# Two-layer attention and routing kernel: values' tail product on four tiles of the array, second layer's side rows made by POOL

## The chip, the cores and the metric

One core of one Trainium2 chip runs the whole program. The metric is device time in microseconds (us), the median of three runs. TensorE is called PE here, VectorE DVE, ScalarE ACT, GpSimd POOL and the queue that issues most DMAs SP.

## The reference

The input x is 4 batches of 2048 tokens of width 512. Two layers follow each other, each an attention over a short context and a feed-forward part:

```
x = x + xcond(layernorm(x), ctx, ...)     # layer 0: 16 heads of 32, 154 keys per batch
x = x + moe(layernorm(x))                 # 32 experts, 8 for a token
x = x + xcond(layernorm(x), ctx, ...)     # layer 1, own weights
x = x + light_and_heavy(layernorm(x))     # light MLP for all, heavy MLP for 512 routed tokens of a batch

def xcond(q_in, ctx, tau, delta):
    q, k, v = heads(q_in @ Wq.T + bq), heads(ctx @ Wk.T + bk), heads(ctx @ Wv.T + bv)
    p = softmax((q @ k.T * tau + delta) / sqrt(32))      # over 154 keys
    return merge(p @ v) @ Wo.T + bo
```

The change touches only the two attentions (the product `p @ v`) and, in layer 1, the layernorm whose rows go to the light and heavy part.

## The kernel before

The program is a sequence of phases: keys and values of layer 0, `token_phase` for layer 0, expert slots and experts, `token_phase` for layer 1, the mixed phase and the heavy phase. `token_phase` walks over 16 turns of 512 tokens (four tiles of 128). A turn has 16 units, one for each group g of four heads and each tile t (unit u = 4g + t), and 32 slots `at`, two for each unit. The order of all work on every engine is written out by hand: each engine has a function `turn` that goes through the slots in order, and tables of slot numbers (`V`, `OL`, `RES`, `NZ`, `PT`, `OO` and others, lines 349 to 380) say in which slot a piece of work stands. Turn i works on three sets of tokens at once: the attention of turn i, the output projection of turn i - 1, the side rows of turn i - 2; V, PT, OO and OL name slots of this turn for groups 0 and 1 (and 2 for PT), and of the next turn for the rest.

One unit goes through the engines like this. PE makes the scores (L980, four heads, banks 0 to 2 of PSUM); DVE takes the maximum (L684); ACT makes the exponentials of four heads and their sums (L915); DVE the reciprocal (L699); POOL multiplies the 128 main keys (L609) and the 26 tail keys (L611) by it; PE turns the four heads of the main keys into bank 4 (L992) and the 4 x 26 = 104 tail columns into bank 5 (L993); DVE, in two of 16 units ACT, copies bank 4 to `pTm` (L707, L861). PE may use bank 4 again for unit v only when all copies up to v - 1 are done, and makes the last head of the scores of unit u only when ACT has read the first head of unit u - 1 (the semaphore `shared`). When the four units of a group are done, ACT copies bank 5 to `pTt` (L854), and PE makes the values (`values`, L1003 and L1006): one fp32 product of 104 rows, whose left operand `vt` is block-diagonal (rows of four heads, zeros off their own columns), and four fp32 products of 128 rows and 32 columns, one per head, onto the same bank 7. A product in fp32 is two MATMUL instructions in the trace. ACT (L849) and DVE (L726) take the result out as high and low part. Bank 6 holds queries and projections in turn.

In layer 1, DVE does in slots 3, 7, 10 and 13 the normalised side rows of turn i - 2 (`normed(1, "s", ...)`, L675 with output `z`) from `xs`, which the next residual (L716, slot 12, one buffer) overwrites tile by tile; they all are on DVE, so no semaphore stands between them. In the slots around it POOL has L654 (`xbo`, slots 6, 10, 16, 22) and L602 (`q_low`, slots 26, 1, 11, 15). POOL's 16 turns are a loop with waits against registers.

The constants at the top of the file that matter: `KTAIL` = 26, `HG` = 4 heads in a group, `TG` = 4 tiles, `GTOK` = 512 tokens of a turn.

Of the kernel before, what the change touches and what calls it, by code (L numbers as in the profile page):

```python
# [20 lines left out]
P = 128  # L21
B, SEQ, D = 4, 2048, 512
NTOK = B * SEQ
KEYS = 154
# [4 lines left out]
TROWS = HG * KTAIL  # L29
# [16 lines left out]
UNITS = TG * GROUPS  # L46
KROWS = 3 * DK + 2
# [121 lines left out]
def store_tails(sp, scr, l, k, s):  # L169

    for h in range(HG):
        sp.dma_start(scr[f"vt{l}"].rearrange("b (n h) (g e d) -> h (b n) g e d", h=HG, e=HG, d=DK)[h, :, :, h, :],
                     k["vt"][:].rearrange("n (g e d) -> n g e d", e=HG, d=DK)[:, :, h, :]).then_inc(s["stored"], 16)


KV_STORED = 16 * (2 * 3 * HG + 2 + HG)
# [29 lines left out]
def key_value_phase(nc, a, scr, c):  # L206

    with ExitStack() as ctx:
# [6 lines left out]
        zero = sb("zero", [TROWS, D])  # L215
# [6 lines left out]
        def _(sp):  # L222
# [7 lines left out]
            for l in range(2):  # L230
                sp.dma_start(scr[f"vt{l}"].rearrange("b t d -> t b d"),
                             zero[:].unsqueeze(1).to_broadcast([TROWS, B, D])).then_inc(s["cleared"], 16)
# [61 lines left out]
def token_phase(nc, l, a, scr, c, x_in, x_rows):  # L294
    gate = l == 0
    with ExitStack() as ctx:
# [6 lines left out]

        wq, wo = operands("wq", [P, DC, D]), operands("wo", [P, DC, D])
        bq, bo = sb("bq", [P, DC]), sb("bo", [P, D])
        kst = sb("kst", [KROWS, GROUPS, HG * KEYS], F32R)
        vm, vt = sb("vm", [P, D]), sb("vt", [TROWS, D])
# [7 lines left out]
        tails = sb("tails", [P, 4, TROWS])  # L315
        pTm, pTt = sb("pTm", [P, 2, HG, D]), sb("pTt", [TROWS, D])
        negmax, total, inv = (sb(n, [P, UNITS, HG]) for n in ("negmax", "total", "inv"))
        stat, mv = sb("stat", [P, 2, TG, 6]), sb("mv", [P, 2, TG, 2])
# [8 lines left out]
        else:  # L327
# [7 lines left out]
                 "q_mm q_out q_high q_low scored negmax shared exped inv normed p_mm pTm pTt pv oT_high oT_out proj resid "  # L335
# [4 lines left out]
        T_BANK, A_BANK, B_BANK = 3, 6, 7  # L340
# [8 lines left out]
        V = (15, 24, 2, 7) if gate else (15, 23, 3, 6)  # L349
# [4 lines left out]
        OL = (23, 30, 4, 9) if gate else (17, 27, 5, 9)  # L354
# [8 lines left out]
        NZ = (0, 0, 1, 1) if gate else (3, 7, 10, 13)  # L363
# [3 lines left out]
        PT = (11, 19, 28, 3) if gate else (11, 19, 27, 4)  # L367
        OO = (16, 26, 2, 7) if gate else (15, 24, 4, 7)
# [39 lines left out]

        def o_bank(j, t):

            return (A_BANK, 0, 1, 2)[t] if last(j) else A_BANK
# [20 lines left out]
        def load_values(sp, j, g):  # L432
# [4 lines left out]
            sp.dma_start(vt[:, g * P:(g + 1) * P], scr["vt%d" % l][b, :, g * P:(g + 1) * P]).then_inc(s[f"v_in{g}"], 16)  # L437
# [139 lines left out]
        def _(pool):  # L577
            pool.memset(half[:], -0.5).then_inc(s["ready"], 1)
            pool.memset(eps[:], EPS).then_inc(s["ready"], 1)
            if not gate:  # L580
                pool.memset(z[:, :, D:XS], 0.0).then_inc(s["ready"], 1)
                pool.memset(c["z_last"][:, :, D:XS], 0.0).then_inc(s["ready"], 1)
            pool.wait_ge(s["ready"], 2 if gate else 4)
# [21 lines left out]
            def normalize(i, v):  # L605
# [3 lines left out]
                pool.tensor_tensor(main, main, inv[:, v, :].unsqueeze(2).to_broadcast([P, HG, P]),  # L609
                                   ALU.mult).then_inc(s["normed"], 1)  # L610
                pool.tensor_tensor(tails[:, v % 4, :].rearrange("p (n h) -> p h n", h=HG), tail,  # L611
                                   inv[:, v, :].unsqueeze(2).to_broadcast([P, HG, KTAIL]),
                                   ALU.mult).then_inc(s["normed"], 1)

            def turn(i, par, prev2, prev, cur, nxt, nxt2, before, batch):
# [14 lines left out]
                for st in range(UNITS):  # L630
# [3 lines left out]
                    for at in (2 * st, 2 * st + 1):  # L634
# [21 lines left out]
            turns(pool, turn)  # L656

        @block.vector
        def _(dve):
# [37 lines left out]
            def inverse(i, v):  # L697
                dve.wait_ge(s["exped"], UNITS * i + v + 1)
                dve.reciprocal(inv[:, v, :], total[:, v, :]).then_inc(s["inv"], 1)  # L699
# [10 lines left out]
            def residual(j, t):  # L710
# [12 lines left out]
            def o_low(i, par, g):  # L723
                dve.wait_ge(s["oT_high"], GROUPS * i + g + 1)
                k = o_slot(par, g)
                dve.tensor_tensor(oT[1][:, k, :], ps[:, B_BANK, :], oT[0][:, k, :].bitcast(F32),  # L726
# [34 lines left out]
            def turn(i, par, prev2, prev, cur, nxt, nxt2, before, batch):  # L761
# [3 lines left out]
                for at in range(2 * UNITS):  # L765
# [45 lines left out]
                    if prev2:  # L811
# [1757 lines left out]
```

## Time and profile before

| what | value |
|---|---|
| median of three runs | 3376.84 us (3376.42 to 3385.39) |
| the profiled execution, its own time | 3380.68 us |
| its span, first to last instruction | 3378.9 us |
| granted TensorE clock, mean over the span | 0.978 of full speed |
| busy share PE, DVE, ACT, POOL | 95%, 81%, 46%, 62% |
| one turn of layer 0, of layer 1 | about 52.6 us, about 50.5 us |

A busy PE means that some matmul is in flight; its instructions overlap, so times of the PE work are best read from start to start in the timeline. The timeline merges neighbouring instructions of one line (`x4`); its first two columns are start and duration of the merged stretch in us.

### The profile page before, as it was taken

What the parts mean: (1) busy time and instruction counts of PE and PEld (TensorE: products, weight loads), DVE (VectorE), ACT (ScalarE), POOL (GpSimd) and SP (SyncE); (2) the same over time, 40 slices, a digit from 0 to 9 for tenths busy, and PEclk for the clock granted to TensorE, in tenths of its full rate; (3) what the DMA queues carried; (4) which work ended last, traced back from release to release, by engine and by line L of the source; (5) the groups of instructions that cost most, each with busy time, mean ns of one, the idle gap of its engine ahead of it and who ended that gap; (6) DMA issues with size and microseconds to landing.
All of it is one profiled execution on the core that took longest, in us unless ns stands there. A gap on an engine that the chain in (4) does not pass through costs nothing. (4 is left out here: it accounts for less than half of the span.)

```text
span 3378.9 us, 55655 instructions
## 1 busy us (share of the span) xinstructions
PE 3197.8 (95%) x17324; PEld 2506.5 (74%) x17324; DVE 2735.5 (81%) x5290; ACT 1560.9 (46%) x5449; POOL 2081.7 (62%) x2335
## 2 busy tenths in 40 slices
PE   7999999999979999999999699999999969999998
PEld 5677777777648888888888577777777757778886
DVE  4788888888677887888887379999999879967775
ACT  1766767667521111111111377777777745321111
POOL 1776666766536777777777477777777753443333
PEclk8999999999979999999999899999999989999999
DMA  7345454454465667676766544555554457730111
GB/s 218 100 137 173 122 166 140 137 174 125 141 174 154 171 169 175 170 166 166 176 164 156 112 128 133 160 163 143 151 172 135 138 164 286 274 103 13 26 13 25
DMA packets 284781, 490.97 MB, mean 145 GB/s; under 512 B 54018, under 2 KB 74818, under 8 KB 283778
## 3 DMA queue, kind: packets, MB, share of 16 engines
q1 hardware_dynamic: 243698, 408.87, 39.6%
q0 software_dynamic: 32256, 77.65, 12.4%
q10 hardware_dynamic: 8592, 1.57, 0.3%
q8 instruction: 116, 1.90, 0.2%
q14 instruction: 119, 0.97, 0.1%
HBM read 250.32 MB, written 136.96 MB: 115 GB/s over the span
## 5 line engine op out<-in xcount | busy, mean ns | idle before, releaser
L915 ACT ACTIVATE c_pr<-ps,t_negmax 128x154 f32<-128x154 f32 x1024 | 385.7, 393 | 180.8 <-DVE t_negmax L684 178.6
L684 DVE TENSOR_REDUCE t_negmax<-ps 128x4 f32<-128x616 f32 x512 | 403.6, 788 | 53.3 <-PE ps L980 52.6
L915 ACT ACTIVATE t_pr<-ps,t_negmax 128x154 f32<-128x154 f32 x1024 | 385.6, 393 | 105.8 <-DVE t_negmax L684 101.4
L707 DVE COPY t_pTm<-ps 128x512 f32<-128x512 f32 x448 | 306.0, 683 | 127.3 <-PE ps L993 123.0
L609 POOL TENSOR_TENSOR t_pr<-t_pr,t_inv 128x512 f32<-128x512 f32 x256 | 275.7, 1077 | 191.0 <-DVE t_inv L699 189.3
L609 POOL TENSOR_TENSOR c_pr<-c_pr,t_inv 128x512 f32<-128x512 f32 x256 | 272.0, 1063 | 196.4 <-DVE t_inv L699 195.0
L980 PE MATMUL ps<-t_kst,t_stack 98*128 98x154 f32 x2048 | 353.0, 291 | 26.3 <-DMA t_stack<-t_q_low 10.1
L980 PEld LDWEIGHTS ps<-t_kst,t_stack 98*128 98x128 f32 x2048 | 279.6, 194 | 38.9 <-issue 17.8
L81 PE MATMUL ps<-e_xT_high,e_wgu_high 128*128 128x512 f32 x768 | 302.4, 394 | 1.4 <-DVE e_xT_low L1508 1.4
L83 PE MATMUL ps<-e_xT_high,e_wgu_low 128*128 128x512 f32 x768 | 299.6, 390 | 0.0
L82 PE MATMUL ps<-e_xT_low,e_wgu_high 128*128 128x512 f32 x768 | 299.4, 390 | 0.0
L1618 ACT ACTIVATE e_sig<-ps 128x512 f32<-128x512 f32 x96 | 57.5, 599 | 516.2 <-PE ps L83 516.2
L81 PE MATMUL ps<-t_xnT_high,t_wq_high 128*128 128x512 f32 x512 | 221.3, 432 | 19.1 <-ACT t_qT L842 18.4
L2286 POOL TENSOR_TENSOR h_w_low<-c_hw,h_w_high 128x512 fp32r<-128x512 f32 x64 | 89.9, 1405 | 229.3 <-DVE h_w_high L70 229.3
L81 PE MATMUL ps<-t_wo_high,t_oT_high 128*128 128x512 f32 x512 | 217.9, 426 | 0.0
L602 POOL TENSOR_TENSOR t_q_low<-t_qT,t_q_high 128x512 fp32r<-128x512 f32 x128 | 170.7, 1334 | 68.8 <-DVE t_q_high L70 68.8
L915 ACT ACTIVATION_READ_ACCUMULATOR t_pr<-ps,t_negmax 128x1 f32 x1024 | 213.0, 208 | 0.0
L915 ACT ACTIVATION_READ_ACCUMULATOR c_pr<-ps,t_negmax 128x1 f32 x1024 | 212.4, 207 | 0.0
L1480 POOL TENSOR_TENSOR e_wd_low<-c_wd_in,e_wd_high 128x512 fp32r<-128x512 f32 x96 | 131.1, 1394 | 128.9 <-DVE e_wd_high L70 128.9
L83 PE MATMUL ps<-t_xnT_high,t_wq_low 128*128 128x512 f32 x512 | 203.0, 396 | 0.0
L82 PE MATMUL ps<-t_xnT_low,t_wq_high 128*128 128x512 f32 x512 | 202.2, 395 | 0.0
L83 PE MATMUL ps<-t_wo_high,t_oT_low 128*128 128x512 f32 x512 | 201.4, 393 | 0.0
(373 smaller groups left out, 9320.9 us busy)
## 6 DMA issues: line engine op xcount, KB each, us to landing
t_stack<-t_q_high SPq DMA_DIRECT2D x1016, 64.0 KB, 2.0
c_wgu_in<-in_gate_upT SPq DMA_DIRECT2D x32, 1536.0 KB, 6.4
t_stack<-t_q_low SPq DMA_DIRECT2D x512, 64.0 KB, 2.0
x_dram<-c_wide_rows SPq DMA_DIRECT2D x32, 1024.0 KB, 7.8
c_wd_in<-in_downT SPq DMA_DIRECT2D x32, 768.0 KB, 4.5
t_xbo<-in_x SPq DMA_DIRECT2D x16, 1024.0 KB, 7.0
xw_dram<-t_z SPq DMA_DIRECT2D x16, 1024.0 KB, 5.3
t_xbo<-x_dram SPq DMA_DIRECT2D x16, 1024.0 KB, 11.0
```

Source lines behind the costliest of these rows:

```text
L81: pe.matmul(out, left[0], right[0], start=start, stop=False)
L82: pe.matmul(out, left[0], right[1], start=False, stop=False)
L83: return pe.matmul(out, left[1], right[0], start=False, stop=stop)
L602: pool.tensor_tensor(qlow[:, n % 2, :], qT[:, n % 2, :], qhigh[:, n % 2, :].bitcast(F32), ALU.subtract).then_inc(s["q_low"], 1)
L609: pool.tensor_tensor(main, main, inv[:, v, :].unsqueeze(2).to_broadcast([P, HG, P]), ALU.mult).then_inc(s["normed"], 1)
L684: dve.tensor_reduce(negmax[:, u, :], flat[:, at:at + HG * APART].rearrange("p (h n) -> p h n", h=HG)[:, :, 0:KEYS], AX, ALU.max, negate=Tr ...
L707: dve.tensor_copy(pTm[:, g % 2, :, t * P:(t + 1) * P], ps[:, 4, :].rearrange("p (h n) -> p h n", h=HG)).then_inc(s["pTm"], 1)
L915: op = act.activation(pr[:, u % 4, h, :], flat[:, col:col + KEYS], ACT.Exp, bias=negmax[:, u, h:h + 1], accum_out=total[:, u, h:h + 1])
L980: mm = pe.matmul(flat[:, at:at + KEYS], stack[:, HG * (g % 2) + h, t * P:(t + 1) * P], kst[:, g, h * KEYS:(h + 1) * KEYS], start=True, sto ...
L1480: pool.tensor_tensor(wd[q][1][:, f, :], wd_in[:, f, :], wd[q][0][:, f, :].bitcast(F32), ALU.subtract).then_inc(s["wd_low"], 1)
L1618: act.activation(sig[:, (FC * q + f) % 2, :], ps[:, b, :], ACT.Silu).then_inc(s["silu"], 1)
L2286: pool.tensor_tensor(w1[1][:, m % RING], c["hw1"][:, :, f * P:(f + 1) * P], w1[0][:, m % RING].bitcast(F32), ALU.subtract).then_inc(s["w1" ...
```

## The change

For the tail keys, the group's four heads are now two pairs. `vt` holds 52 rows for a pair (two heads of 26), twice: in partitions 0 to 51 and 64 to 115 (both copies loaded, one DMA more for each load of values). POOL writes the tails of a unit with the pairs apart, in one of 8 places of 116 columns. For tiles 2 and 3 of a turn the heads stand in swapped order (`place`), so that each half of the tokens finds its pairs in other partitions. PE turns the tails of a group in one go (`tail_transposes`, slots `TT`), no longer unit by unit, and its wait on `oT_out` stands there since bank 5 now also holds results. The tail product is four products of 52 rows, 64 columns and 256 tokens; the main product eight of 128 rows, 32 columns and 256 tokens; the results go to the first halves of banks 5 and 6. In layer 1 the side rows are made by POOL (`side_rows`, slots 2, 5, 8, 12) and the residual of tile 0 waits for all four; POOL's turns of layer 1 are written out. `inv` is gone (the reciprocal overwrites `total`), and several slots move.

```diff
-        V = (15, 24, 2, 7) if gate else (15, 23, 3, 6)
+        V = (15, 24, 2, 7) if gate else (15, 23, 1, 7)
+        TT = (12, 20, 30, 5) if gate else (12, 20, 29, 5)
-        OL = (23, 30, 4, 9) if gate else (17, 27, 5, 9)
+        OL = (18, 27, 4, 9) if gate else (17, 26, 3, 9)
-        NZ = (0, 0, 1, 1) if gate else (3, 7, 10, 13)
+        NZ = (0, 0, 1, 1) if gate else (2, 5, 8, 12)
-        PT = (11, 19, 28, 3) if gate else (11, 19, 27, 4)
-        OO = (16, 26, 2, 7) if gate else (15, 24, 4, 7)
+        PT = (12, 20, 30, 5) if gate else (12, 20, 29, 5)
+        OO = (16, 25, 2, 7) if gate else (15, 24, 2, 7)
...
+            for r in (0, HIGH):
+                sp.dma_start(vt[r:r + PROWS, g * P:(g + 1) * P],
+                             scr["vt%d" % l][b, :, g * P:(g + 1) * P]).then_inc(s[f"v_in{g}"], 16)
...
+            def side_rows(j, t):
+                pool.wait_ge(s["s_rstd"], j + 1)
+                if t == 0 and j < NG - 1:
+                    reached(pool, s["z_stored"], 16 * j)
+                pool.tensor_scalar(z_of(j)[:, t, 0:D], xs[:, t, :], mv[:, 1, t, 0:1], rstd[:, 1, t:t + 1],
+                                   ALU.subtract, ALU.mult).then_inc(s["xl"], 1)
...
+                        if at in NZ and prev2 and not gate:
+                            side_rows(i - 2, NZ.index(at))
...
-            turns(pool, turn)
+            turns(pool, turn) if gate else unrolled(turn)
...
                 if t == 0:
                     reached(dve, s["x_stored"], 16 * j)
+                    if not gate:
+                        reached(dve, s["xl"], TG * j)
                 dve.tensor_tensor(xs[:, t, :], ps[:, o_bank(j, t), :], xbo[:, t, :], ALU.add).then_inc(s["resid"], 1)
...
-                pe.transpose(ps[0:TROWS, 5, t * P:(t + 1) * P], tails[:, v % 4, :],
-                             ident[:]).then_inc(s["p_mm"], 1)
+            def tail_transposes(i, g):
+                pe.wait_ge(s["normed"], 2 * (UNITS * i + TG * g + TG))
+                reached(pe, s["oT_out"], GROUPS * i + g)
+                for t in range(TG):
+                    at = (HIGH + PROWS) * ((TG * g + t) % 8)
+                    mm = pe.transpose(ps[0:HIGH + PROWS, 5, t * P:(t + 1) * P], tails[:, at:at + HIGH + PROWS], ident[:])
+                mm.then_inc(s["tail_mm"], 1)
...
-                pe.matmul(ps[:, B_BANK, :], vt[:, g * P:(g + 1) * P], pTt[:], start=True, stop=False,
-                          skip_group_check=True)
-                for h in range(HG):
-                    mm = pe.matmul(ps[h * DK:(h + 1) * DK, B_BANK, :], vm[:, g * P + h * DK:g * P + (h + 1) * DK],
-                                   pTm[:, g % 2, h, :], start=False, stop=True, skip_group_check=True)
+                for half in range(2):
+                    for q in range(2):
+                        r = HIGH * (q if half == 0 else 1 - q)
+                        pe.matmul(ps[HIGH * q:HIGH * (q + 1), 5 + half, 0:HALF],
+                                  vt[r:r + PROWS, g * P + HIGH * q:g * P + HIGH * (q + 1)],
+                                  pTt[r:r + PROWS, half * HALF:(half + 1) * HALF], start=True, stop=False,
+                                  skip_group_check=True)
+                for half in range(2):
+                    for h in range(HG):
+                        mm = pe.matmul(ps[h * DK:(h + 1) * DK, 5 + half, 0:HALF],
+                                       vm[:, g * P + h * DK:g * P + (h + 1) * DK],
+                                       pTm[:, g % 2, h, half * HALF:(half + 1) * HALF], start=False, stop=True,
+                                       skip_group_check=True)
                 mm.then_inc(s["pv"], 1)
```

`HIGH` is 64, `PROWS` 52, `HALF` 256. The two printouts below are of DVE in a layer 1 turn, slots 11 to 13, before and then with the change. In brackets stand the semaphores waited for; layer 1 reuses those of layer 0, so they carry layer 0's names: what is called `t0_z_mm` is `xl`, the count of side rows made.

```order
L684 TENSOR_REDUCE t_negmax<-ps 128x4 [waits t0_shared]
L699 RECIPROCAL t_inv<-t_total 128x4 [waits t0_normed]
L675 TENSOR_SCALAR t_x<-t_x,t_mv,t_rstd 128x512 [waits t0_xbo]
L716 TENSOR_TENSOR c_wide_rows<-ps,t_xbo 128x512 [waits t0_stacked0,t0_xnT_high,t0_s_stats]
L707 COPY t_pTm<-ps 128x4x128 [waits t0_pTt]
L684 TENSOR_REDUCE t_negmax<-ps 128x4 [waits t0_shared]
L699 RECIPROCAL t_inv<-t_total 128x4 [waits t0_normed]
L663 BN_STATS t_stat<-c_wide_rows 128x6 [waits t0_s_mv]
L675 TENSOR_SCALAR t_z<-c_wide_rows,t_mv,t_rstd 128x512 [waits t0_z]
```

```order
L714 TENSOR_REDUCE t_negmax<-ps 128x4 [waits t0_shared]
L729 RECIPROCAL t_total<-t_total 128x4 [waits t0_normed]
L705 TENSOR_SCALAR t_x<-t_x,t_mv,t_rstd 128x512 [waits t0_xbo]
L748 TENSOR_TENSOR c_wide_rows<-ps,t_xbo 128x512 [waits t0_stacked0,t0_z_mm,t0_xnT_high,t0_s_stats]
L737 COPY t_pTm<-ps 128x4x128 [waits t0_pTm]
L714 TENSOR_REDUCE t_negmax<-ps 128x4 [waits t0_shared]
L729 RECIPROCAL t_total<-t_total 128x4 [waits t0_normed]
L693 BN_STATS t_stat<-c_wide_rows 128x6 [waits t0_s_mv]
```

The side row behind the statistics is gone from DVE, and the residual (L716, now L748) has one wait more.

POOL in the same turn with the change, slots 8 to 13 (the rows of L640 are the side rows of tiles 2 and 3):

```order
L640 TENSOR_SCALAR t_z<-c_wide_rows,t_mv,t_rstd 128x512 [waits t0_z]
L624 TENSOR_TENSOR t_pr<-t_pr,t_total 128x4x128 [waits t0_p_mm]
L630 TENSOR_TENSOR t_tails<-t_pr,t_total 128x2x52
L684 TENSOR_TENSOR t_xbo<-t_xbo,t_bo 128x512 [waits t0_ones]
L624 TENSOR_TENSOR t_pr<-t_pr,t_total 128x4x128 [waits t0_p_mm]
L630 TENSOR_TENSOR t_tails<-t_pr,t_total 128x2x52 [waits t0_pTt]
L617 TENSOR_TENSOR t_q_low<-t_qT,t_q_high 128x512 [waits t0_scored]
L640 TENSOR_SCALAR t_z<-c_wide_rows,t_mv,t_rstd 128x512 [waits t0_z]
```

Before, the same stretch had only the rows of the normalisation, of `xbo` and of `q_low`. The fourth side row stands behind the normalisation of unit 4, which waits for DVE's reciprocal of slot 11, and behind `q_low`.

## Rows read from the trace of the kernel before

**Rows 1.** The page, busy time, share of the span and instructions.
```profile
PE 3197.8 (95%) x17324; PEld 2506.5 (74%) x17324; DVE 2735.5 (81%) x5290; ACT 1560.9 (46%) x5449; POOL 2081.7 (62%) x2335
```

**Rows 2.** Windows: one turn of layer 0, one of layer 1 (length, busy us).
```profile
core 0: us, PE busy (x) PEld busy (x) DVE busy (x) ACT busy (x) POOL busy (x), PEclk, DMA share, GB/s
405.00:457.90 52.90, 52.16 (x326) 39.20 (x325) 45.25 (x99) 36.34 (x150) 35.15 (x45) 1.00 0.50 144
2340.13:2390.59 50.46, 49.07 (x300) 37.16 (x299) 48.25 (x100) 40.07 (x160) 38.33 (x46) 1.00 0.54 157
```

**Rows 3.** Waits of PE in eleven turns of layer 1 (total, times, longest).
```profile
PE ps L81 <- ACT t_qT L842: 9.0, 11, 0.8
PE ps L980 <- ACT t_pr L915: 5.2, 11, 0.5
```

**Rows 4.** Groups by line, PE: the tail product, two instructions each.
```profile
L1003 PE MATMUL ps<-t_pTt,t_vt 104*128 104x512 f32 x256 | 135.8, 612 | 1.6 <-DVE t_oT_low L726 1.4
```

**Rows 5.** Timeline of one group's values, layer 0 (three neighbouring windows).
```profile
410.14 1.02 PE L1003 MATMUL ps<-t_pTt,t_vt 104*128 104x512 f32 x2
...
410.58 0.59 PE L1003 MATMUL ps<-t_pTt,t_vt 104*128 104x512 f32 x1
...
411.10 0.16 PEld L1006 LDWEIGHTS ps<-t_pTm,t_vm 128*32 128x32 f32 x8 [0.76 <-issue]
411.10 0.64 PE L1006 MATMUL ps<-t_pTm,t_vm 128*32 128x512 f32 x4
...
411.55 0.61 PE L1006 MATMUL ps<-t_pTm,t_vm 128*32 128x512 f32 x4
...
412.09 0.66 PE L992 MATMUL ps<-ident,c_pr 128*128 128x128 f32 x4
```

**Rows 6.** Timeline of DVE, layer 1, slots 11 to 13.
```profile
2390.08 0.16 DVE L699 RECIPROCAL t_inv<-t_total 128x4 f32<-128x4 f32 x1
2390.16 0.51 DVE L675 TENSOR_SCALAR t_x<-t_x,t_mv,t_rstd 128x512 f32<-128x512 f32 x1
2390.59 0.68 DVE L716 TENSOR_TENSOR c_wide_rows<-ps,t_xbo 128x512 f32<-128x512 f32 x1
2391.19 0.68 DVE L707 COPY t_pTm<-ps 128x512 f32<-128x512 f32 x1
2391.79 0.78 DVE L684 TENSOR_REDUCE t_negmax<-ps 128x4 f32<-128x616 f32 x1
```

**Rows 7.** Timeline of POOL, the same stretch.
```profile
2390.32 1.26 POOL L609 TENSOR_TENSOR t_pr<-t_pr,t_inv 128x512 f32<-128x512 f32 x1
...
2391.86 1.29 POOL L602 TENSOR_TENSOR t_q_low<-t_qT,t_q_high 128x512 fp32r<-128x512 f32 x1
2393.10 1.05 POOL L609 TENSOR_TENSOR t_pr<-t_pr,t_inv 128x512 f32<-128x512 f32 x1
```

**Rows 8.** Timeline of PE and ACT, the same stretch: unit 4's transposes, unit 7's scores.
```profile
2390.97 0.61 PE L965 MATMUL ps<-ident,t_x 128*128 128x128 f32 x4
2391.34 0.48 PE L81 MATMUL ps<-t_wo_high,t_oT_high 128*128 128x512 f32 x1
...
2392.83 0.60 PE L992 MATMUL ps<-ident,t_pr 128*128 128x128 f32 x4
...
2393.30 0.55 PE L980 MATMUL ps<-t_kst,t_stack 98*128 98x154 f32 x3
...
2392.61 0.43 ACT L915 ACTIVATE t_pr<-ps,t_negmax 128x154 f32<-128x154 f32 x1
```

**Rows 9.** Timeline: a slow POOL row of this size; DVE's side row of slot 7.
```profile
2305.07 1.75 POOL L654 TENSOR_TENSOR t_xbo<-t_xbo,t_bo 128x512 f32<-128x512 f32 x1
...
2383.68 1.26 DVE L675 TENSOR_SCALAR t_z<-c_wide_rows,t_mv,t_rstd 128x512 f32<-128x512 f32 x1
```

**Rows 10.** SP: issue of a load of `vt`; stores of side rows, us to landing.
```profile
2317.45 0.43 SPq L437 DMA_DIRECT2D t_vt<-vt_dram  x1
...
xs_dram<-t_z SPq DMA_DIRECT2D x14, 1032.0 KB, 4.5
```

More of the change, by code:

```diff
@@ L169, in store_tails @@
 def store_tails(sp, scr, l, k, s):
-    for h in range(HG):
-        sp.dma_start(scr[f"vt{l}"].rearrange("b (n h) (g e d) -> h (b n) g e d", h=HG, e=HG, d=DK)[h, :, :, h, :],
-                     k["vt"][:].rearrange("n (g e d) -> n g e d", e=HG, d=DK)[:, :, h, :]).then_inc(s["stored"], 16)
-KV_STORED = 16 * (2 * 3 * HG + 2 + HG)
+    for b in range(B):
+        for e in range(2):
+            sp.dma_start(scr[f"vt{l}"][b, e * KTAIL:(e + 1) * KTAIL, :].rearrange("n (q e d) -> n q e d", e=2, d=DK)[:, :, e, :],
+                         k["vt"][b * KTAIL:(b + 1) * KTAIL, :].rearrange("n (q e d) -> n q e d", e=2, d=DK)[:, :, e, :]
+                         ).then_inc(s["stored"], 16)
+KV_STORED = 16 * (2 * 3 * HG + 2 + 2 * B)
 KV_JOBS = 13
@@ L314, in token_phase @@
         pr = c["pr"] if gate else sb("pr", [P, 4, HG, KEYS])
[L315 to L318, printed above, removed]
+        tails = sb("tails", [P, 8 * (HIGH + PROWS) + HIGH - PROWS])
+        pTm, pTt = sb("pTm", [P, 2, HG, D]), sb("pTt", [HIGH + PROWS, D])
+        total, mv = sb("total", [P, UNITS, HG]), sb("mv", [P, 2, TG, 2])
         ve, rstd = sb("ve", [P, 2, TG]), sb("rstd", [P, 2, TG])
@@ L407, in last, with place, halves @@
             return isinstance(j, int) and j == NG - 1
+        def place(h, t):
+            return h if t < TG // 2 else (h + 2) % HG
+        def halves(v):
+            return v.rearrange("p (b n) -> p b n", b=2)
         def o_bank(j, t):
@@ L579, in _ @@
             pool.memset(eps[:], EPS).then_inc(s["ready"], 1)
+            pool.memset(tails[:], 0.0).then_inc(s["ready"], 1)
             if not gate:
@@ L582, in _ @@
                 pool.memset(c["z_last"][:, :, D:XS], 0.0).then_inc(s["ready"], 1)
[L583 removed]
+            pool.wait_ge(s["ready"], 3 if gate else 5)
             def rstd_of(which, kind, n):
@@ L914, in turn @@
                             col = BASE[u % 2] + h * APART
-                            op = act.activation(pr[:, u % 4, h, :], flat[:, col:col + KEYS], ACT.Exp,
-                                                bias=negmax[:, u, h:h + 1], accum_out=total[:, u, h:h + 1])
+                            to = place(h, u % TG)
+                            op = act.activation(pr[:, u % 4, to, :], flat[:, col:col + KEYS], ACT.Exp,
+                                                bias=negmax[:, u, h:h + 1], accum_out=total[:, u, to:to + 1])
                             if n == 0:
@@ L1116, in turn @@
                         streamed(st)
+                    if at in TT[:3] and cur:
+                        tail_transposes(i, TT.index(at))
+                    if at == TT[3] and prev:
+                        tail_transposes(i - 1, GROUPS - 1)
                     if at in V[:2] and cur:
```

58 lines of the change are left out of this document (30 added, 28 removed).

## The prediction

> **What bounds the kernel now.** The page comes first: PE is busy for 95% of the span, DVE for 81%, POOL for 62% [rows 1]. The windows then tell the two attention stages apart. A turn of layer 0 lasts 52.90 us and PE is busy for 52.16 of it, DVE for 45.25. A turn of layer 1 lasts 50.46 us with PE busy for 49.07 and DVE for 48.25, which is 96%; POOL has 38.33 [rows 2]. So both stages go at PE's pace, layer 0 with room on the others, layer 1 with next to none on DVE. The view of waits names the little that PE loses in layer 1: once a turn 0.8 us for a query that ACT takes out, once a turn 0.5 us for an exponential [rows 3]. Both end in chains from PE over DVE and ACT that the change leaves alone. What matters is therefore, first, how many us of PE the values take, and second, whether a new wait reaches PE.
>
> **The values on PE.** There are 128 groups (256 instructions of the tail product, two each) [rows 4]. In the timeline a group's values take 1.95 us, from 410.14 to 412.09: the tail product's instructions start at 410.14 and 410.58, the main product's in two rounds of four at 411.10 and 411.55, the next work at 412.09 [rows 5]. A round over 512 tokens is thus 0.44 us, the second tail round 0.52 and the second main round 0.54. I read the extra 0.08 and 0.10 us as the price of changing the array's tiling, since before 411.10 no weights are loaded for 0.76 us and then all eight loads fit in 0.16 us. Those four-at-once rounds also show that four column tiles work side by side.
>
> The new tail product has half the tokens per round. If its four tiles run side by side too, it is two rounds of 0.22 us. The main product becomes four rounds of 0.22. Tiling now changes three times: into 64 x 64, into 128 x 32, and back. Sum: 0.08 + 2 x 0.22 + 0.08 + 4 x 0.22 + 0.10 = 1.58 us, 0.37 less than 1.95; I take 0.36. Bounds: 0.44 if the first change is free, 0.28 if each of the four added round starts costs 0.02. Over 128 groups: **-46 us** (-56 to -36). The tail transposes stay 16 a turn and cost about the 0.37 us per four that L965 shows from 2390.97 to 2391.34 [rows 8], now in one piece, before in four: nothing.
>
> The rule that speaks against this stands in the Trainium skill, TensorEngine Tiling (Array Packing), Restrictions and Gotchas: different row tiles cannot use one PSUM bank at the same time. Here both row tiles write bank 5 at once, and both write bank 6, though in other partitions. By that rule the tail product would not shrink; it is rival C. No row before the change has two row tiles at once.
>
> **The new wait in layer 1.** DVE sheds four side rows a turn, of 1.26 us the one shown [rows 9]. DVE is not what PE waits for at those slots, so this alone gives nothing. But the residual of slot 12 now waits for four side rows on POOL, and the fourth stands behind unit 4's normalisation and behind `q_low`. I walk through one turn. DVE's reciprocal of unit 4 ends at 2390.24 [rows 6]; POOL's normalisation starts at 2390.32, `q_low` behind it at 2391.86 with 1.29, and POOL is free at 2393.1 [rows 7]. POOL has shown no one-input operation of this size: the nearest are 1.05 us (L609) below and 1.75 us above [rows 7, 9], nearest in work is L609, and I take 1.1. The side row ends at 2394.2, so the residual starts at 2394.3 and not at 2390.59: 3.7 us late. Queued behind it on DVE are the copy of unit 3 (`pTm`) and unit 6's maximum. With the 0.60 us from L716 to L707 and 0.68 for the copy, the copy ends at 2395.6. PE wants it for unit 4's transposes, at 2392.83 [rows 8], or at 2393.15 with the four tail transposes now in front: a wait of 2.5 us. The maximum starts at 2395.5, the first exponential 0.82 us later (2391.79 to 2392.61), ends at 2396.75, and the last head of unit 7's scores, ready at about 2396.45, waits 0.3 more. Against that, DVE without its side rows of slots 7 and 10 reaches slot 11 earlier; most of their time it then waits for PE's scores instead, and I count 0.3 us. So 2.5 us a turn. It happens in turns 2 to 15, 14 times: **+35 us** (1.9 to 3.2 us a turn: +27 to +45). The lower end has no wait in the scores and an idle POOL port, the upper end a side row of 1.75 us.
>
> The Trainium skill (GPSIMD Engine Reference, Elementwise, side-by-side cycle accounting) gives 769 ns for 512 elements in POOL's best loop with one input; an estimate by that has the turn wait 0.3 us less, 4 us in all.
>
> **The rest.** POOL rises from 38.33 to about 43 us a turn. Its side rows of slots 2, 5 and 8 fill time in which it waited for DVE: nothing. At slot 2 it also waits for the last store of side rows, which lands 4.5 us after its issue late in the turn before [rows 10]; one normalisation is queued behind it, which PE wants only some two units later. In layer 0 the tail transposes of slot 5 wait for DVE's low part of slot 4, which follows the values of slot 2 with a unit of PE's work between: nothing. The second copy of `vt` adds 0.43 us of SP for each of 16 loads a layer [rows 10], ahead of query stacks in a few turns: +1 us. The last turn's side rows, now on POOL with DVE's dot products beside them: +1 us at most. The unrolled loop takes away register instructions that POOL did while it waited: nothing.
>
> **Sum.** -46 + 35 + 2 = -9 us. The profiled execution took 3380.68 us, so 3371.7 by it; it was 3.84 us over the median of 3376.84, so I predict 3368 us for the median.
>
> **Rivals.** What a measurement of this kernel can tell from no change is about 0.3%, 10 us: faster is below 3366.7, slower above 3387.
>
> A, the forecast: own range 3350 to 3387, from -56 + 27 + 2 to -36 + 45 + 2, rounded. Chance 0.5. Nearly half of it lies under 3366.7.
>
> B, the wait is there on DVE but PE makes it good: once PE has stood still, ACT, DVE and POOL have caught up, and the waits of 0.8 and 0.5 us a turn [rows 3] vanish, with some of the 0.3 in the scores. That gives back up to 1.8 us in 14 turns, 25 us: 3343. For it speaks DVE's lower load; against it that those waits are chains that start at PE. Chance 0.2.
>
> C, the two row tiles do not write one bank at the same time. The tail product is then two pairs in turn, four rounds of 0.22, as long as before, with one more change of tiling: 0.08 us more per group and not 0.36 less. That is +10 and not -46: 3424, slower. It decides as soon as the tail costs over 0.75 us a group instead of the 0.52 forecast with its entry. The token halves in two banks are made so that no partition of a bank is written twice, which speaks against it. Chance 0.15.
>
> D, POOL becomes late at more places. At 43 of 50 us, with DVE on the same SBUF ports (L675 on the same size takes 0.51 us in one place and 1.26 in another [rows 6, 9]), the normalisations slip and PE waits 1 us more in 14 turns: 3382, up to 3400. Chance 0.15.
>
> **Chances.** Faster by over 0.3%: 0.23 of A and B's 0.2, 0.43. Within: 0.25 of A, 0.05 of D, 0.30. Slower: C, 0.1 of D, a rest of A, 0.27. The range 3335 to 3422 holds A and D, most of B, and reaches to C.
>
> **What would show it.** In the changed trace, a group's values should take 1.6 us from the first tail instruction to the next work; about 2.0 means C. Layer 0's turn should fall from 52.6 to about 51.2 us. In layer 1 the residual should be DVE's longest wait, some 3.7 us once a turn, on POOL's L640, with PE waiting about 2.5 us on the `pTm` copy; the turn should be 51 to 52 us, longer than before. If layer 1's turn is shorter than 50.4 us, the walk through slot 12 is wrong. If L640 takes over 1.5 us, or PE waits for POOL's normalisation, D is at work.

## The result and the profile after

The changed kernel took **3503.44 us** (median of four runs, 3500.74 to 3505.62), the kernel before beside it 3379.26 us. The ratio is 1.0359 with a 95% interval of 1.0345 to 1.0373: 124 us slower, far outside the range of 3335 to 3422.

The page of the changed kernel, busy time by engine, answers to [rows 1]. PE does as much as before, in a span 120 us longer.

```profile
PE 3200.0 (91%) x19116; PEld 2544.1 (73%) x19116; DVE 2691.4 (77%) x5226; ACT 1562.4 (45%) x5449; POOL 2191.2 (63%) x2401
```

The windows of one turn of layer 0 and one of layer 1, the counterparts of [rows 2]:

```profile
core 0: us, PE busy (x) PEld busy (x) DVE busy (x) ACT busy (x) POOL busy (x), PEclk, DMA share, GB/s
405.00:457.36 52.36, 50.92 (x380) 39.63 (x380) 45.17 (x99) 36.05 (x149) 34.74 (x44) 1.00 0.51 146
2282.55:2341.53 58.98, 50.48 (x352) 38.83 (x352) 45.50 (x95) 40.14 (x158) 45.16 (x49) 0.96 0.43 126
```

Layer 0 has hardly gained, layer 1 has lost over 8 us a turn. From here on a turn is the distance between two residuals of tile 0, taken over ten turns of layer 1. For the kernel before these are the starts 2086.51 and 2593.02, so 50.65 us; for the changed kernel they are these two rows of DVE's timeline, so 59.10 us:

```profile
2105.50 0.69 DVE L748 TENSOR_TENSOR c_wide_rows<-ps,t_xbo 128x512 f32<-128x512 f32 x1 [5.87 <-POOL t_z L640]
...
2696.47 0.69 DVE L748 TENSOR_TENSOR c_wide_rows<-ps,t_xbo 128x512 f32<-128x512 f32 x1 [5.87 <-POOL t_z L640]
```

The difference of 8.45 us, in 14 turns, makes 118 of the 124 us. The first residual of layer 1 is only 3.4 us later than before.

PE's waits from 2086 to 2643 us, the same stretch as [rows 3] (some nine and a half turns here, eleven there):

```profile
PE ps L82 <- DVE c_wide_rows L748: 48.9, 10, 4.9
PE ps L82 <- ACT t_qT L872: 21.7, 27, 1.0
PE ps L1011 <- ACT t_pr L946: 8.8, 18, 0.8
```

Three things are to be seen. A wait of 4.9 us once a turn for DVE's residual is new, and it is a projection product of PE (L82) that waits, not a transpose. The wait for a query (`t_qT`) comes three times a turn, before once. The wait for an exponential comes twice, before once. Only the first has to do with the side rows.

Timeline of one turn's slots 11 and 12, all engines:

```profile
2217.96 0.60 PE L996 MATMUL ps<-ident,t_x 128*128 128x128 f32 x4
...
2219.25 1.26 POOL L617 TENSOR_TENSOR t_q_low<-t_qT,t_q_high 128x512 fp32r<-128x512 f32 x1
2220.50 2.07 POOL L640 TENSOR_SCALAR t_z<-c_wide_rows,t_mv,t_rstd 128x512 f32<-128x512 f32 x1
...
2222.70 0.69 DVE L748 TENSOR_TENSOR c_wide_rows<-ps,t_xbo 128x512 f32<-128x512 f32 x1 [5.87 <-POOL t_z L640]
2223.31 0.68 DVE L737 COPY t_pTm<-ps 128x512 f32<-128x512 f32 x1
...
2223.45 0.80 PE L82 MATMUL ps<-t_wo_high,t_oT_high 128*128 128x512 f32 x1 [4.89 <-DVE c_wide_rows L748]
...
2224.04 0.63 PE L83 MATMUL ps<-t_wo_low,t_oT_high 128*128 128x512 f32 x1
2224.47 0.63 PE L84 MATMUL ps<-t_wo_high,t_oT_low 128*128 128x512 f32 x1
```

The projection of tile 1 uses the bank that the residual of tile 0 empties. It stands right behind the x transposes, so PE stops at 2218.56 and not, as my walk had it, only at the transposes of unit 4. And when PE runs again, the second and third product of the next tile start 0.43 us apart, where products follow each other after 0.23 us elsewhere. Windows of the same place, the stop and what follows:

```profile
2217.90:2223.40 5.50, 0.66 (x7) 0.42 (x4) 0.70 (x2) 1.07 (x2) 4.67 (x5) 0.94 0.14 36
2223.40:2228.00 4.60, 4.55 (x15) 3.89 (x16) 2.65 (x5) 2.93 (x12) 1.36 (x2) 0.50 0.06 14
```

The granted clock is 0.50 (1.2 GHz) for the 4.6 us after the stop. So each stop costs twice: the standing itself, and some 2 us more because the work behind it goes at half speed (how this is summed stands further down). Before, three windows of 10 us from 2340 to 2370 all show 1.00.

The values came out as forecast. Timeline of PE at a group's values, counterpart of [rows 5]:

```profile
412.03 0.40 PE L84 MATMUL ps<-t_wo_high,t_oT_low 128*128 128x512 f32 x1
412.36 0.66 PE L1043 MATMUL ps<-t_pTt,t_vt 52*64 52x256 f32 x8
412.95 1.07 PE L1049 MATMUL ps<-t_pTm,t_vm 128*32 128x256 f32 x16
413.95 0.44 PE L1021 MATMUL ps<-ident,c_pr 128*128 128x128 f32 x2
```

From the first tail instruction to the next work they take 1.59 us instead of 1.95. The four tiles do run side by side. What I did not count is the entry: from the last product to the tail's start it is 0.33 us here, where before a product is followed after 0.23 us. Summed from the start of each instruction to the start of the next, over ten turns of layer 1, the values take 6.38 us a turn and took 7.84 before, 0.36 less for each of the four groups. With the entry, 0.09 us more for each group, the saving is 0.27 us a group.

### The profile page after: what moved, and what is told of

Read it like the earlier page. It is cut to its first block and busy times, and to the rows that moved or that the text cites. A ratio compares the mean times of both kernels' runs of the same rounds, so it can differ in the third digit from the quotient of the medians.

```text
span 3498.9 us, 59172 instructions
## 1 busy us (share of the span) xinstructions
PE 3200.0 (91%) x19116; PEld 2544.1 (73%) x19116; DVE 2691.4 (77%) x5226; ACT 1562.4 (45%) x5449; POOL 2191.2 (63%) x2401
## 3 DMA queue, kind: packets, MB, share of 16 engines
q10 hardware_dynamic: 8592, 1.57, 0.3%
## 5 line engine op out<-in xcount | busy, mean ns | idle before, releaser
L624 POOL TENSOR_TENSOR t_pr<-t_pr,t_total 128x512 f32<-128x512 f32 x256 | 269.8, 1054 | 214.4 <-DVE t_total L729 213.5
L624 POOL TENSOR_TENSOR c_pr<-c_pr,t_total 128x512 f32<-128x512 f32 x256 | 272.0, 1063 | 188.1 <-DVE t_total L729 187.5
L82 PE MATMUL ps<-e_xT_high,e_wgu_high 128*128 128x512 f32 x768 | 301.9, 393 | 1.4 <-DVE e_xT_low L1557 1.4
L82 PE MATMUL ps<-t_wo_high,t_oT_high 128*128 128x512 f32 x512 | 227.8, 445 | 71.5 <-DVE c_wide_rows L748 67.6
L82 PE MATMUL ps<-t_xnT_high,t_wq_high 128*128 128x512 f32 x512 | 222.3, 434 | 33.7 <-ACT t_qT L872 32.6
L84 PE MATMUL ps<-t_wo_high,t_oT_low 128*128 128x512 f32 x512 | 208.8, 408 | 0.0
L83 PE MATMUL ps<-t_wo_low,t_oT_high 128*128 128x512 f32 x512 | 208.4, 407 | 0.0
```

Source lines behind the costliest of these rows:

```text
L82: pe.matmul(out, left[0], right[0], start=start, stop=False)
L83: pe.matmul(out, left[0], right[1], start=False, stop=False)
L84: return pe.matmul(out, left[1], right[0], start=False, stop=stop)
L624: pool.tensor_tensor(main, main, total[:, v, :].unsqueeze(2).to_broadcast([P, HG, P]), ALU.mult).then_inc(s["normed"], 1)
```

## The experiments

Theory W says that the loss is the residual's wait for POOL; theories of the values, of slots and of DVE were set beside it as the results asked for them.

**rows_on_dve.** The side rows go back to DVE, the rest of the change stays.

```diff
-        NZ = (0, 0, 1, 1) if gate else (2, 5, 8, 12)
+        NZ = (0, 0, 1, 1) if gate else (3, 7, 10, 13)
...
-                    if not gate:
-                        reached(dve, s["xl"], TG * j)
...
-                        if at in NZ and prev2 and not gate:
-                            side_rows(i - 2, NZ.index(at))
...
+                                normed(1, "s", j, xs, z_of(j), "z" if gate else "xl", (t,))
```

> The changed kernel with the side rows of layer 1 back on DVE (slots 3, 7, 10, 13, no new wait on the residual); values, tails, stores of vt and the unrolled POOL stay. Theory W (the loss is the residual's wait for four POOL rows): it is gone. Layer 0 and the start stay as in the changed kernel, 3 to 4 us behind before at the first residual of layer 1. In layer 1 PE has 1.4 us less work a turn, but DVE was busy for 48.25 of 50.46 us, so a turn can only fall to about 50.0: 3372 to 3382 us. Theory V (the values' new form costs time of itself in layer 1, by its tail transposes in one piece and bank 5 shared): a turn above 51 us, the time over 3395.

Measured: 3400.71 us, ratio 1.0046 (1.0029 to 1.0063) to the kernel before. The long wait is gone, but this is slower than before, not the same: the turn is 52.42 us. Theory W explains most of the loss, and theory V holds for the rest: the values' part, which I had at -46 us, is itself a loss of 16 us. PE's waits in the same stretch:

```profile
PE ps L82 <- ACT t_qT L870: 23.3, 30, 1.0
PE ps L1009 <- ACT t_pr L944: 10.7, 22, 0.8
```

**before_pool_rows.** The other half alone: the kernel before with the side rows on POOL.

```diff
-        NZ = (0, 0, 1, 1) if gate else (3, 7, 10, 13)
+        NZ = (0, 0, 1, 1) if gate else (2, 5, 8, 12)
...
+                    if not gate:
+                        reached(dve, s["xl"], TG * j)
...
+                        if at in NZ and prev2 and not gate:
+                            side_rows(i - 2, NZ.index(at))
...
-            turns(pool, turn)
+            turns(pool, turn) if gate else unrolled(turn)
```

> The kernel before with nothing but the side rows moved to POOL (slots 2, 5, 8, 12), the residual's wait for all four and POOL's layer 1 turns written out. Theory W: nearly the whole loss of layer 1 is here, the turn goes from 50.5 to 59 us or a little over (it has the old values too, but PE stands still anyway): 3490 to 3515 us, POOL's side row about 2.1 us each. Theory V: well under 3450.

Measured: 3490.07 us, ratio 1.0309 (1.0292 to 1.0326), a turn of 58.14 us. The side rows on POOL cost 105 us by themselves; with the 16 us of rows_on_dve that makes 121 of 124. Rows of its PE waits:

```profile
PE ps L81 <- DVE c_wide_rows L728: 49.2, 10, 5.2
PE ps L1002 <- POOL t_tails L611: 4.6, 7, 0.7
```

The second row is new as well: PE stands for a normalisation that POOL makes late. That is rival D's mechanism, with 0.5 us a turn.

**wait_per_tile.** The changed kernel, but the residual of a tile waits for that tile's side row only.

```diff
-                    if not gate:
-                        reached(dve, s["xl"], TG * j)
+                if not gate and j:
+                    dve.wait_ge(s["xl"], TG * (j - 1) + t + 1)
```

> The changed kernel, but the residual of tile t waits for the side row of tile t of the turn before alone, not tile 0 for all four. Side rows stay on POOL with their 2.08 us. Theory W: at slot 12 the first row (slot 2) is long made, the wait is gone; POOL has 38.3 + 8.4 = 46.7 us of work in a turn and is not the bound, PE has 1.4 us less than before: the turn is 49.5 to 50.5 us, the time 3355 to 3385. Rival P (POOL itself is too full between slots 0 and 12, so that its normalisations reach PE late whatever the residual waits for): the turn stays at 53 us or more, over 3415, with PE or DVE waiting on L624 or L630.

Measured: 3411.88 us, ratio 1.0078 (1.0061 to 1.0095), a turn of 52.74 us. One condition gives back 92 of the 124 us: tile 0 never needed the rows of tiles 1 to 3. The number lies between the ranges of W and P, just under P's. It misses W's because W still held the values for a gain; against rows_on_dve (52.42) it is 0.3 us a turn. That rest is rival P in small, POOL's normalisation late once a turn:

```profile
PE ps L1021 <- POOL t_tails L630: 7.9, 10, 0.8
```

**pool_one_operation.** How much is the length of POOL's row?

```diff
-                pool.tensor_scalar(z_of(j)[:, t, 0:D], xs[:, t, :], mv[:, 1, t, 0:1], rstd[:, 1, t:t + 1],
-                                   ALU.subtract, ALU.mult).then_inc(s["xl"], 1)
+                pool.tensor_scalar(z_of(j)[:, t, 0:D], xs[:, t, :], mv[:, 1, t, 0:1], None,
+                                   ALU.subtract).then_inc(s["xl"], 1)
```

> The changed kernel, but the side row on POOL only subtracts the mean; the product with rstd is left out, so that its rows aren't the reference's. If POOL's 2.08 us are two passes of about 1 us, one for each scalar: the row takes 1.0 to 1.1 us, the residual of tile 0 waits under 2 us a turn, the time falls to 3425 to 3450. If they are the cost of a form with scalars by partition as such: still about 2 us, and within 10 us of the changed kernel.

Measured: 3483.4 us in one run, a turn of 58.08 us, the residual's wait 4.11 us. The view of one tile's instructions on POOL (minimum, median and maximum in ns), first of the changed kernel:

```profile
L640 POOL TENSOR_SCALAR t_z<-c_wide_rows,t_mv,t_rstd x60: 2065/2077/2135, 2024.8 to 2853.6; 128x512 f32<-128x512 f32 x60
```

and of this one:

```profile
L640 POOL TENSOR_SCALAR t_z<-c_wide_rows,t_mv x60: 1556/1565/1786, 2022.0 to 2839.2; 128x512 f32<-128x512 f32 x60
```

Neither expectation holds: the second scalar, with its operation, costs 0.51 us of 2.08. Rows shorter by 2.0 us a turn in all shorten the turn by 1.0 us only. The length is the smaller part; where POOL's work stands counts for more. In the changed kernel POOL's timeline is full without a gap from 2206.77 to 2222.57, with 14 instructions: three side rows, four normalisations of two instructions each, two `xbo` and `q_low`. A row that must be ready at slot 12 ends a queue of 15.8 us.

**rows_on_act.** As wait_per_tile, with the side rows on ACT.

```diff
-                        if at in NZ and prev2 and not gate:
-                            side_rows(i - 2, NZ.index(at))
...
+                act.activation(z_of(j)[:, t, 0:D], xs[:, t, :], ACT.Identity, bias=ve[:, 1, t:t + 1],
+                               scale=rstd[:, 1, t:t + 1]).then_inc(s["xl"], 1)
```

> As wait_per_tile, but the four side rows are made by ACT (one activation with scale and bias by partition, slots 3, 7, 11, 13); POOL only makes the shift (three operations of 128x4 a turn). ACT had 40 of 50 us in layer 1 and gets about 0.6 us for each row. Theory W and rival P both: no long wait is left; the turn is 49.2 to 50 us, 3350 to 3375. Under P this is better than wait_per_tile by 40 us or more, under W by less than 15.

Measured: 3394.99 us, ratio 1.0033 (1.002 to 1.0045), a turn of 51.63 us. It missed its range of 3350 to 3375, since the values' loss is still in it. It is 17 us better than wait_per_tile (by the medians; its six runs spread from 3389 to 3400), between the two expectations, and its waits for `t_qT` (23.6 us, 29 times) and `t_pr` (10.5, 22) are those of rows_on_dve. With the side rows off DVE and POOL (POOL only makes the small shift), something of the values' part still costs 1 us a turn against before.

**before_new_slots.** The kernel before with three tables of the change.

```diff
-        V = (15, 24, 2, 7) if gate else (15, 23, 3, 6)
+        V = (15, 24, 2, 7) if gate else (15, 23, 1, 7)
...
-        OL = (23, 30, 4, 9) if gate else (17, 27, 5, 9)
+        OL = (18, 27, 4, 9) if gate else (17, 26, 3, 9)
...
-        OO = (16, 26, 2, 7) if gate else (15, 24, 4, 7)
+        OO = (16, 25, 2, 7) if gate else (15, 24, 2, 7)
```

> The kernel before, old values and tails, with nothing changed but the tables V, OL and OO, which take the numbers of the changed kernel (layer 1: values of groups 2 and 3 in slots 1 and 7 for 3 and 6, low parts in 17, 26, 3 for 17, 27, 5, high part of group 2 in slot 2 for 4; layer 0: low part of group 0 and 1 in 18 and 27 for 23 and 30). Theory S (the layer 1 loss that is left with the side rows on DVE is made by these slots: the values of slot 3 had covered ACT's copy of a query, the low part of slot 27 had stood behind the maximum): PE waits about 2.3 us a turn for t_qT and 1.0 for t_pr, instead of 0.8 and 0.5, the turn of layer 1 is 52 us or more, the time 3405 to 3425. Rival T (it is the tail transposes in one piece or the new products that cost): the time stays within 8 us of before.

Measured: 3407.05 us, ratio 1.0068 (1.005 to 1.0086), a turn of 52.04 us, so theory S holds for the time and the turn. Of its two waits only the one for a query grows, to 1.9 us a turn. PE's waits:

```profile
PE ps L81 <- ACT t_qT L842: 19.3, 31, 0.9
PE ps L980 <- ACT t_pr L915: 5.2, 11, 0.5
```

Five moved slots in layer 1 and three in layer 0 cost 24 us, with old values and old side rows. The timeline of rows_on_dve shows the place: the products of a query end, ACT must take it out before the next may use the bank, and where the values of slot 3 had stood in between, PE now waits.

```profile
2392.57 0.50 PE L82 MATMUL ps<-t_xnT_high,t_wq_high 128*128 128x512 f32 x1 [1.01 <-ACT t_qT L870]
```

The wait for an exponential stays at 0.5 us once a turn here; that it is 0.8 us in rows_on_dve, with a second one of 0.2 beside it, these slots alone don't make.

**third_bank.** Why were the slots moved? In the change, bank 5 holds both the tail transposes and half of the results, so a group's results must be gone before the next tails can be turned, and everything between moves forward. This kernel takes rows_on_dve and puts the second half of groups 1 to 3 of layer 1 into the bank of the x transposes, which stands empty then. With the banks renumbered so that two neighbours are read together, and waits on PE that guard the borrowed bank, the old slots are back.

```diff
-        T_BANK, A_BANK, O_BANKS = 3, 7, slice(5, 7)
+        T_BANK, A_BANK = (3, 7) if gate else (7, 3)
...
+            return (5, 6) if gate or g == 0 else (6, T_BANK)
...
-        V = (15, 24, 2, 7) if gate else (15, 23, 1, 7)
+        V = (15, 24, 2, 7) if gate else (15, 23, 3, 6)
...
-        OL = (18, 27, 4, 9) if gate else (17, 26, 3, 9)
+        OL = (18, 27, 4, 9) if gate else (17, 27, 5, 9)
```

> The changed kernel with side rows on DVE (as rows_on_dve), and in layer 1 the values' second half of groups 1 to 3 goes to the bank of the x transposes, which stands empty then, instead of the bank of the tail transposes (group 0 still uses that one). The slots of layer 1 are those of the kernel before (V 15, 23, 3, 6; OL 17, 27, 5, 9; OO 15, 24, 4, 7; PT and TT 11, 19, 27, 4). Layer 0 as in the changed kernel. Theory S (the shared bank forces the early slots, and these cost): the waits for t_qT and t_pr fall back to 0.8 and 0.5 us a turn, and the shorter values show: a turn of 49.5 to 50.2 us against 52.2 in rows_on_dve, the time 3358 to 3376. Rival D (DVE, busy for 48.3 us of a turn, is the bound as soon as PE has less): 50.4 to 50.8, 3375 to 3385. Rival T (the new products or transposes cost of themselves): over 51, over 3388.

Measured: 3377.47 us, ratio 0.9986 (0.9977 to 0.9996), a turn of 50.68 us. Against rows_on_dve that is 1.7 us a turn: the shared bank and its slots were the values' loss. The waits now:

```profile
PE ps L82 <- ACT t_qT L879: 9.1, 11, 0.8
PE ps L1018 <- ACT t_pr L953: 8.3, 11, 0.8
PE ps L1018 <- issue: 5.3, 5, 1.6
```

The last row, `issue`, is time for which the profile names no releaser; L1018 are the scores, which read the query stacks that SP's DMAs bring. Before, that row was:

```profile
PE ps L980 <- issue: 2.0, 4, 0.8
```

The mean turn shows no gain, 50.65 before and 50.68 here, in the range of rival D. But the ten turns are not alike: their median is 50.21 us, before 50.47. The three longest are 52.97, 51.57 and 51.37 us, every fourth turn, and each has a stop of 1.3 to 1.6 us at a query stack; before, the three longest are 51.26, 50.99 and 50.82. In the longest the clock falls behind the stop (2131.8 to 2133.4 us), which it doesn't in the second:

```profile
2136.00:2139.00 3.00, 3.00 (x13) 2.62 (x12) 2.39 (x5) 1.37 (x9) 2.56 (x4) 0.57 0.26 66
```

Summed from start to start and with waits apart, a mean turn has 1.45 us less of values than before, and against it 0.65 more of waits (half of it at the query stacks, the other half nearly all for exponentials), 0.5 more of products (mostly the entry), 0.2 of scores and 0.1 of transposes. So the gain is there and is spent again within PE's turn; what DVE has to do with it is for the next run.

**third_bank_act_rows.** third_bank with ACT's side rows and the wait per tile of rows_on_act.

> third_bank with the side rows on ACT (0.82 us each in rows_on_act, slots 3, 7, 11, 13) and the residual of tile t waiting for the side row of tile t alone. In third_bank the turn of layer 1 stayed at 50.7 us although the values take 1.15 us less of PE, and DVE was the engine without room. Theory D (DVE is the bound of third_bank): with four rows of 0.5 to 1.3 us taken from it, the turn falls to 49.3 to 49.8 us, the time to 3355 to 3366. Rival (what third_bank lost is in chains that start at PE, as the waits for t_qT and t_pr): the turn stays at 50.4 to 50.7, 3372 to 3380.

Measured: 3373.35 us, ratio 0.9975 (0.9965 to 0.9985), a turn of 50.16 us. The time is in the rival's range, the turn between the two: relief of DVE brings 0.5 us a turn (medians of the ten turns: 49.70 against 50.21), about half of what theory D asked for. The waits for `t_qT` (9.0 us, 11 times), `t_pr` (8.3, 11) and at the query stacks (4.6, 3) stay as in third_bank. The first two are chains that start at PE, the rival's; the third is for DMAs, which neither theory had.

**before_act_rows.** The same side rows on ACT in the kernel before.

> The kernel before, its values and slots kept, with only the side rows of layer 1 on ACT (slots 3, 7, 11, 13), the wait per tile and POOL's layer 1 turns written out. If PE was the bound of layer 1 before, as its 49.1 busy of 50.5 us said: within 5 us of before, a turn of 50.3 to 50.6 us. If DVE was: the turn falls under 50, the time to 3370 or less, and the values are not what makes third_bank_act_rows fast.

Measured: 3377.9 us, ratio 0.9988 (0.9979 to 0.9998), a turn of 50.63 us. So before the change PE was the bound of layer 1 and DVE, at 96%, was not. By the turns of these single traces DVE's load counts only once PE has less: side rows on ACT bring 0.02 us a turn here and 0.52 in third_bank. The medians of the whole time do not show this: they fall by 4.7 us here and by 4.1 there, within each other's noise.

**two_stores.** At the start, the first residual of layer 0 came at 148.54 us instead of 141.94.

```diff
-    for b in range(B):
-        for e in range(2):
-            sp.dma_start(scr[f"vt{l}"][b, e * KTAIL:(e + 1) * KTAIL, :].rearrange("n (q e d) -> n q e d", e=2, d=DK)[:, :, e, :],
-                         k["vt"][b * KTAIL:(b + 1) * KTAIL, :].rearrange("n (q e d) -> n q e d", e=2, d=DK)[:, :, e, :]
-                         ).then_inc(s["stored"], 16)
+    for e in range(2):
+        sp.dma_start(scr[f"vt{l}"][:, e * KTAIL:(e + 1) * KTAIL, :].rearrange("b n (q e d) -> b n q e d", e=2, d=DK)[:, :, :, e, :],
+                     k["vt"][:].rearrange("n (q e d) -> n q e d", e=2, d=DK)[:, :, e, :]).then_inc(s["stored"], 16)
```

> As rows_on_dve, but the tails of the values are stored to vt_dram by two DMAs for each layer (all batches in one) instead of eight. If the start's loss (the first residual 6 to 7 us later than before) comes from the eight stores, which took 7.0 us of SP's queue for 2.2: 4 to 6 us less than rows_on_dve, and a first residual at 143 to 146 us. If it is the second copy of vt or something behind it: within 2 us of rows_on_dve.

Measured: 3401.36 us, ratio 1.0053 (1.0036 to 1.0071): the same as rows_on_dve. SP's rows say why. First of the kernel before (issue of the stores, then the first load of the next phase, which waits for their landing):

```profile
46.03 2.18 SPq L172 DMA_DIRECT2D vt_dram<-kv_vt  x4
50.59 0.40 SPq L445 DMA_DIRECT2D t_bq<-in_bq  x1
```

then of two_stores:

```profile
45.81 2.44 SPq L173 DMA_DIRECT2D vt_dram<-kv_vt  x2
53.40 0.37 SPq L457 DMA_DIRECT2D t_bq<-in_bq  x1
```

In the changed kernel the eight stores are issued from 46.12 to 53.14 us and `t_bq` follows at 55.31. Two large stores are issued in 2.4 us but land 5.2 us later, where four landed in 2.4. The first residual is at 148.80 us, outside the 143 to 146 expected. The first residual comes at 148.5 to 152.7 us in all kernels with the new values and at 141.9 to 143.7 with the old, and of this the stores explain up to 4.7 us; what delays it behind `t_bq` was not isolated.

**act_rows_four_stores.** third_bank_act_rows with four stores, one for each head of a group over all batches.

> As third_bank_act_rows, with the tails stored to vt_dram by four DMAs over all batches (one for each head of a group) instead of eight. two_stores issued fast but landed 5 us after its last issue. With four of the size that the kernel before has, issue and landing should be as before: t_bq is issued at 51 us and not at 55.3, and the time is 4 us less than third_bank_act_rows.

Measured: 3368.75 us, ratio 0.9963 (0.995 to 0.9976), and `t_bq` at 53.27 us, not 51. It is 4.6 us under third_bank_act_rows as forecast, though the intervals of the two overlap, and `t_bq` comes only 2.3 us earlier than there (55.58). Four stores of the old size, in another order of elements, were issued in 3.6 us and landed 4.0 us later, not 2.4. **This version is faster than both kernels**, by 0.4% than the one before.

**one_copy_of_vt.** What keeps layer 0's gain small?

```diff
-            for r in (0, HIGH):
+            for r in ((0,) if j else (0, HIGH)):
```

> As act_rows_four_stores, but the second copy of vt (partitions 64 to 115) is loaded for the first batch only; for the other batches it keeps the first batch's rows, so that their values are not the reference's. If the second copy's DMAs on SP are why layer 0 gains only 0.3 us a turn (the query stacks and xbo come later, with PE waiting 0.3 us a turn for each of the two): the turn of layer 0 falls from 52.4 to 51.9 us or less. If not: it stays within 0.1 of 52.4, and the cause is the slots or the shared bank.

Measured: 3367.61 us in one run; ten turns of layer 0 take 52.18 us each, against 52.33 in act_rows_four_stores, between the two expectations. The second copy's DMAs make up at most 0.15 us of it, and that is no more than traces with the same work in layer 0 differ (52.33 to 52.53). The waits for POOL's tails fall from 0.19 to 0.04 us a turn, while the waits at the query stacks stay. Layer 1 gains 0.24 us a turn, and there the waits at the query stacks fall from 0.54 to 0.27. In the total little of this is left (its one run is 1.1 us under the median of act_rows_four_stores).

## Why the prediction was wrong

**The values on PE: the mechanism right, the size a little off.** A group's values take 1.59 us, forecast 1.58, and rival C, at 0.15 the only mechanism that I had for a loss there, is false: row tiles that write one bank in different partitions run side by side (tail in 0.59 us, C asked for over 0.75). By the rule of the Trainium skill (TensorEngine Tiling (Array Packing), Restrictions and Gotchas) they could not; the trace disagrees for this case. The entry was mis-sized: 0.27 us a group with it instead of 0.36, so -35 us and not -46.

**The step that failed first: the walk through slot 12, by which the residual starts 3.7 us late and PE waits 2.5 us for the `pTm` copy.** In its place stand 5.9 and 4.9 us, for three reasons; the second and third could be had from the kernel before. POOL's row was taken as 1.1 us, from an operation with two tensors; it takes 2.08, above my upper bound of 1.75. I let POOL arrive at slot 11 with nothing queued and put its side rows of slots 2, 5 and 8 at nothing; but the first twelve slots also have to hold its other work, and it ran 15.8 us without a gap. And I looked for the first thing on PE that needs DVE's copy, and overlooked that PE's own projection needs the residual. The Trainium skill (GPSIMD Engine Reference, Elementwise, side-by-side cycle accounting) has 769 ns for 512 elements in the best loop. The trace is far from it: here the form with two scalars takes 2077 ns.

**A term that was missing: the clock after a stop.** I priced a wait by its length. After a stop of 4.9 us the granted clock is 0.50 for 4.6 us. Products, summed from start to start without the waits, take 25.48 us a turn with the stop and 23.74 without (rows_on_dve). So 2.5 us forecast a turn became 7.5 (before_pool_rows against before): 4.9 of standing, 0.5 of waits for POOL's normalisation, and 2.0 of slower work, +105 us, not +35.

**A term put at nothing without a reason: the moved slots.** The sum has no term for the new V, OL and OO of layer 1, and no word on what they had covered. They cost 24 us. The work that had hidden ACT's copy of a query was the very group of values that moved from slot 3 to slot 1. So the values' part lost its gain: -35 from shorter products and +24 from the slots, and up to rows_on_dve's +16 another 27. By the two traces rows_on_dve is 8 us behind at the first residual of layer 0, gains 8 in layer 0 and loses 20 in layer 1. In a turn of layer 1 the values take 1.45 us less; against it stand 2.3 us more of waits (1.5 for queries, 0.5 for exponentials, 0.2 for DVE's copy), 0.5 more of products (mostly the entry), 0.4 of scores and 0.1 of transposes. Of these, before_new_slots has the scores and 1.1 of the queries' 1.5; the rest was not measured alone.

**The small terms.** The store of the tails was overlooked as a part of the change (eight DMAs for four): the next phase starts 4.7 us later. The second copy of `vt` was taken as +1 us and is, on the last version, at most 0.15 us a turn in layer 0 and 0.24 in layer 1, 6 us over all turns by one trace, of which that run's total shows 1; its size stays open.

**Layer 0** was to fall by 1.4 us a turn and fell by 0.3 (52.69 to 52.37). The values do take 1.5 us less a turn there; against it stand 0.6 us more of waits (0.2 to 0.3 each for DVE's copy, the query stacks, POOL's tails and an exponential, less 0.3 for a query), 0.3 of scores, 0.2 of products and 0.1 of transposes. The slots alone make 0.2 of it (52.90 in before_new_slots) and the second copy at most 0.15; the rest was not isolated and stays open.

**The rivals.** B, that PE makes the wait good, did not happen: in before_pool_rows the waits for a query and for an exponential stay at 0.8 and 0.5 us a turn. D named the right sign, L640 over 1.5 us; its own mechanism makes only the 0.5 us a turn for POOL's normalisation, and its price was far too small since the forecast's own wait was. A single bank for all four tiles, which would need no moved slots, was not tried: two row tiles would then write the same partitions of one bank.

## What to carry to other kernels

When work is moved to an engine with room, look at the room in the slots before the deadline, not in the turn, and make each consumer wait for the one row that it overwrites: here that single condition was worth 92 us. When a change moves pieces of an order written by hand to make a buffer fit, price what each piece had been hiding; a second bank for the results, empty at that time, was worth 23 us here, where the faster product alone was worth 35. And price a stop of PE with the slow stretch behind it.

## What the runs showed of the hardware

- POOL's `tensor_scalar` on 128x512 takes 2.08 us with two scalars by partition and 1.57 with one; its product with a broadcast tensor 1.04 (medians of the traces). DVE does the two-scalar form in 0.5 to 1.5 us, ACT (scale and bias) in 0.82.
- Eight instructions of 52 rows, 64 columns and 256 tokens on four tiles take 0.59 us from start to start of the next, with two row tiles writing one bank in other partitions. Entering the tiling costs 0.09 us.
- After PE stood still for 4.9 us the granted clock was 0.50 for 4.6 us, then 0.89 over 7 us and 1.00. After stops of 1.6 and 1.5 us in third_bank it fell once (0.84 over the next 2.6 us, 0.57 over 3 more) and once not at all.
- The same bytes stored by two DMAs instead of four land 5.2 us after their issue instead of 2.4. The number is not all: four in another order of elements land after 4.0 us, eight after 2.2.
